# One decoder block on one core: order of the last block's cross-attention softmax, and who splits the experts' weights

## What is computed

```
x = x + attention(layernorm(x))            # 16 heads, rotary, softmax over 64 keys
x = x + cross_attention(layernorm(x), ctx) # 16 heads, ctx is (32, 64, 64)
x = x + experts(layernorm(x))              # 8 experts, top 2
```

```
scores = einsum('bhsr,bhlr->bhsl', q_r, k_r)
attn   = softmax(scores, axis=-1)
ctx_c  = einsum('bhsl,bld->bhsd', attn, kv_r)
out    = (ctx_c @ w_kc_kv per head) @ Wo.T
...
for i in range(8):
    h = silu(x @ Wg[i]) * (x @ Wu[i])
    output += w_i * (h @ Wd[i])            # w_i is 0 unless expert i is in the token's top 2
```

## Time and profile before

| | us |
|---|---|
| median of 3 runs | 747.36 |
| lowest and highest of the 3 | 743.05, 750.27 |
| profiled execution, its own time | 745.28 |
| its span | 743.5 |
| TensorE matmul busy | 649.7 (87% of the span) |
| VectorE busy | 532.6 (72%) |
| ScalarE busy | 332.5 (45%) |
| GpSimd busy | 230.4 (31%) |
| mean granted TensorE clock, share of full | 0.955 |

### The profile page before, as it was taken

How to read it: one execution, slowest core, us unless ns; L and a number is a source line. 1 busy time by engine, 2 the same in 40 slices (tenths; PEclk the granted TensorE clock), 3 DMA queues, 4 the chain that set the end, 5 groups by cost and what they waited for, 6 DMA issues and landing times.

```text
span 743.5 us, 14956 instructions
## 1 busy us (share of the span) xinstructions
PE 649.7 (87%) x5522; PEld 475.2 (64%) x5522; DVE 532.6 (72%) x1231; ACT 332.5 (45%) x991; POOL 230.4 (31%) x211
## 2 busy tenths in 40 slices
PE   3787999988999999999799997899889887998770
PEld 2466777777786666656666566566555775887660
DVE  4997999995687889478984789936879554443462
ACT  1476999996721135112351123502476453443330
POOL 1121000000027427232385423943253004003454
PEclk9997999997999999999989999999989999999895
DMA  8799900000000000000002000020442223334445
GB/s 300 148 374 420 408 6 2 1 2 2 2 15 15 1 2 2 15 1 1 2 15 82 18 1 1 23 78 2 126 153 72 70 80 114 100 107 120 130 120 177
DMA packets 49910, 61.52 MB, mean 83 GB/s; under 512 B 15536, under 2 KB 42416, under 8 KB 49584
## 3 DMA queue, kind: packets, MB, share of 16 engines
q1 hardware_dynamic: 45104, 50.88, 20.8%
q0 software_dynamic: 3072, 8.39, 3.6%
q10 hardware_dynamic: 1664, 1.31, 0.6%
HBM read 29.37 MB, written 31.20 MB: 81 GB/s over the span
## 4 chain that ended last, share of the span: by engine, by line
PE 64%; DVE 16%; ACT 7%; issue 6%; DMA 3%; POOL 1%; another core or an unknown queue 1%; ACTq 0%; SPq 0%; DVEq 0%; POOLq 0%
PE bank L352 55%; PE bank L361 9%; DVE m L1097 5%; DVE qmax L1311 2%; DVE csum L1320 2%; ACT kbd L1471 1%; ACT vbd L1457 1%; DMA lncol<-in_L_attn_ln_kv_b 1%; DMA gb<-slots,index 1%; ACT ex L1481 1%; DVE qc L1328 1%; ACT xth L1437 1%; POOL slots L1752 1%; DMA slots<-mxhat,index 0%
## 5 line engine op out<-in xcount | busy, mean ns | idle before, releaser
L1097 DVE TENSOR_TENSOR m<-bank,cst 128x512 f32<-128x512 f32 x192 | 120.9, 682 | 36.2 <-PE bank L352 34.6
L1738 POOL TENSOR_TENSOR r<-m,m 128x512 f32<-128x512 f32 x72 | 91.4, 1293 | 121.4 <-DVE m L1097 97.4
L352 PE MATMUL bank<-xth,wbh 128*128 128x512 f32 x192 | 80.8, 421 | 10.1 <-DVE m L1097 10.1
L1593 ACT ACTIVATE ex<-bank,nmax 128x64 f32<-128x64 f32 x256 | 56.0, 334 | 63.7 <-DVE nmax L1314 63.4
L352 PE MATMUL bank<-xtl,wbh 128*128 128x512 f32 x192 | 76.1, 396 | 0.0
L352 PE MATMUL bank<-xth,wbl 128*128 128x512 f32 x192 | 76.1, 396 | 0.0
L1580 ACT ACTIVATE qc<-bank 128x512 f32<-128x512 f32 x32 | 17.4, 596 | 101.0 <-PE bank L352 101.0
L352 PEld LDWEIGHTS bank<-wop,qc 128*128 128x128 f32 x256 | 46.6, 189 | 24.9 <-issue 19.5
L352 PE MATMUL bank<-wop,qc 128*128 128x256 f32 x256 | 62.3, 389 | 0.0
L352 PE MATMUL bank<-r,wqk 64*64 64x512 f32 x512 | 57.7, 594 | 0.0
L1481 ACT ACTIVATE ex<-bank,nmax 128x64 f32<-128x64 f32 x256 | 54.4, 356 | 3.0 <-DVE nmax L999 2.7
(11 more groups left out here) (217 smaller groups left out, 1493.3 us busy)
## 6 DMA issues: line engine op xcount, KB each, us to landing
slots<-cst SPq DMA_DIRECT2D x1, 13312.0 KB, 43.7
xs<-slots SPq DMA_DIRECT2D x46, 128.0 KB
slots<-ys SPq DMA_DIRECT2D x46, 128.0 KB
slots<-cst SPq DMA_DIRECT2D x1, 5120.0 KB, 50.3
wo_s<-in_L_xattn_Wo SPq DMA_DIRECT2D x1, 2048.0 KB, 18.1
wq_s<-in_L_xattn_Wq SPq DMA_DIRECT2D x1, 2048.0 KB, 11.8
wraw<-in_L_ffn_Wg SPq DMA_DIRECT2D x8, 256.0 KB, 4.7
wraw<-in_L_ffn_Wu SPq DMA_DIRECT2D x8, 256.0 KB, 5.0
```

The costliest lines, as they stand in the source:

```text
L352: return e.matmul(o, l, r, start=start, stop=stop, skip_group_check=True)
L1097: last = e.tensor_tensor(m4[n % 2][m][:, :].rearrange("p (b s) -> p b s", s=S), products[half][:, :].rearrange("p (b s) -> p b s", s=S), t ...
L1593: last = e.activation(ex[b % 4][:, (2 * n + odd) * 64:(2 * n + odd + 1) * 64], score_banks(b)[odd][:, n * 64:(n + 1) * 64], ACT.Exp, bias= ...
L1738: last = e.tensor_tensor(rope[n % 6][half][:, :], m4[n % 2][first][:, :], m4[n % 2][second][:, :], op)
```

## The change

Only block 3 and what follows it change; blocks 0 to 2 are issued as before.

- TensorE and ScalarE: in block 3 the transposes of batch `b` move from step `b + 3` to `b + 2` and now stand behind the scores of that step (`LAG[3]` is 2). Contexts and output halves move one step forward, on TensorE and VectorE.
- ScalarE: the high halves are made in the order 0, 1, 2, 3, 5, 4, 7, 6 (`SPLIT_ORDER`), all of them ahead of `x_high(0)`.
- VectorE: low halves of 2, 3, 4 and 6 at steps 8 to 11. Those of 5 and 7 go to GpSimd, at steps 11 and 12, behind its last scatter. A low half waits for the high half's place in `SPLIT_ORDER`.

```diff
+        LAG = (3, 3, 3, 2)
+        SPLIT_ORDER = (0, 1, 2, 3, 5, 4, 7, 6)
+        HIGH_AT = {8: (2,), 9: (3, 5), 10: (4, 7), 11: (6,)}
...
-                for s in range(12):
-                    if 3 <= s < 11:
+                lag = LAG[blk]
+                for s in range(9 + lag):
+                    if lag == 3 and 3 <= s < 11:
                         cross_weights_T(blk, s - 3)
                     if s < 8:
                         cross_scores(blk, s)
                     if s == 1 and blk:
                         route_step(blk - 1, 12)
-                    if s >= 4:
-                        contexts(blk, s - 4)
+                    if lag == 2 and 2 <= s < 10:
+                        cross_weights_T(blk, s - 2)
+                    if s > lag:
+                        contexts(blk, s - lag - 1)
                     if s < AHEAD - 1 and blk < 3:
                         half_products(blk + 1, s + 1)
-                    if s >= 6:
-                        cross_out(blk, OUT_AT[s - s % 2], s % 2)
+                    if s >= lag + 3:
+                        cross_out(blk, (s - lag - 3) // 2, (s - lag - 3) % 2)
...
             def weights_low(n):
                 at = slice(WE * n, WE * (n + 1))
-                w.wait_ge(w_hi, n + 1)
+                w.wait_ge(w_hi, SPLIT_ORDER.index(n) + 1)
                 e.tensor_tensor(wlo[:, at], wraw[:, at], whi[:, at].bitcast(F32), ALU.subtract).then_inc(w_lo, 1)
...
-                    if 4 <= s < 12:
-                        context_out(blk, s - 4)
-                    if s - 2 in OUT_AT:
-                        cross_out(blk, OUT_AT[s - 2])
+                    if 0 <= s - LAG[blk] - 1 < 8:
+                        context_out(blk, s - LAG[blk] - 1)
+                    if s - 2 + 3 - LAG[blk] in OUT_AT:
+                        cross_out(blk, OUT_AT[s + 1 - LAG[blk]])
                     if s == 2 and blk:
                         route_step(blk - 1, 13)
                     if blk == 3 and s == 8:
                         table(0)
-                    if blk == 3 and 9 <= s < 13:
-                        weights_low(s - 7)
+                    if blk == 3 and 8 <= s < 12:
+                        weights_low((2, 3, 4, 6)[s - 8])
...
             x_low(0)
-            weights_low(6)
             cross_out(3, 3)
             x_low(1)
-            weights_low(7)
...
-                    if 3 <= s < 11:
+                    if blk < 3 and 3 <= s < 11:
                         cross_weights_T(blk, s - 3)
                     if s < 8:
                         cross_exp(blk, s)
-                    if blk == 3 and 8 <= s < 12:
-                        weights_high(s - 6)
+                    if blk == 3 and 2 <= s < 10:
+                        cross_weights_T(blk, s - 2)
+                    if blk == 3 and s in HIGH_AT:
+                        for n in HIGH_AT[s]:
+                            weights_high(n)
...
-            weights_high(6)
             x_high(0)
-            weights_high(7)
             x_high(1)
...
                     if blk and 4 <= s < 12:
                         scatter(blk - 1, s - 4)
+                    if blk == 3 and s >= 11:
+                        weights_low((5, 7)[s - 11])
```

More of the change, by code:

```diff
@@ L1753, in scatter, with weights_low @@
                                      in_=mxhat[:, t, :], in_offset=None).then_inc(d_scat, 16)
+            def weights_low(n):
+                at = slice(WE * n, WE * (n + 1))
+                w.wait_ge(w_hi, SPLIT_ORDER.index(n) + 1)
+                e.tensor_tensor(wlo[:, at], wraw[:, at], whi[:, at].bitcast(F32), ALU.subtract).then_inc(w_lo, 1)
             def cross_normed(blk, b):
```

## The result

| | before | changed |
|---|---|---|
| median, us (16 runs each) | 748.56 | 754.39 |
| lowest and highest | 742.17, 754.73 | 749.62, 760.85 |
| profiled execution: span | 743.5 | 755.5 |
| first scores of block 3 at | 533.42 | 537.96 |
| last output half of the loop ends | 570.47 | 577.09 |

The changed kernel is slower. The medians are 5.8 us apart (0.78%); the ratio estimated from all runs is 1.0093, 95% interval 1.0065 to 1.0122, which is 6.9 us.

The account below looks back on a forecast made before the run. It took TensorE's queue and VectorE's low halves, ending close together, to bound the start of the expert rows. Softmax order 0, low halves 4.3 and clock 1.6 gave +5.9 us: 751.2, set up to 751.5; range 748.5 to 753.5, wide 743.8 to 755.5.

Parts of the forecast that it names:

- forecast case: VectorE's and GpSimd's low halves block each other, first tile's output product in time; 751.5 us, chance 0.50.
- TensorE's softmax order: Block 3's loop: work only moves; gain at most 0.66 us and a wait of about 0.8 cancel to 0.
- Scores later: Batch 7's scores come later in block 3; last scatter and first tile's load 0 to 2.8 us later, covered by low halves.
- GpSimd's price: A GpSimd low half of 1536 elements takes 3.75 us, three times its addition of 512 elements.
- No overlap of the five low halves: Before the expert rows, VectorE's three and GpSimd's two low halves add up, ending at 581.25; first `gate_up` 4.3 us later.
- rival A: VectorE's and GpSimd's low halves don't hinder each other; first `gate_up` at 576.3, a gain of 1.5 us; chance 0.15.
- Who goes first: Whether GpSimd's low halves start before VectorE's low half 3, holding up batch 7's copy; both expected at about 568.5.
- rival B: GpSimd goes first and keeps its place between its low halves, delaying VectorE's copy and TensorE's product; +8.9 us, chance 0.25.
- The clock: TensorE idles some 4 us before the first `gate_up`, so its granted clock falls; loss 1.6 us, 0 if idle under 3.
- Rival C: Earlier softmax transposes keep TensorE at full clock from 540 to 546, worth about 3 us; total 748.3, chance 0.10.
- After that: Expert rows, block 3's routing and the combine hang on the first tile and move as a whole.
- The chances: Whole run: slower by over 1% 0.28, faster by over 1% 0.02, within 1% 0.70.

Follow-up runs that it names:

- e1: Against the kernel before, only block 3's softmax order changed, all low halves staying on VectorE; stage 46.77 us against 44.33, ratio 1.0040.
- e7: Changed kernel with GpSimd's two low halves replaced by memsets of the same size, which write and read nothing; stage 44.24 us against the changed kernel's 51.11.
- e10: Changed kernel with each of GpSimd's two low halves made in three pieces of 512 elements; stage 51.99 us against the changed kernel's 51.11.
- e5: Changed kernel with GpSimd's low halves delayed until VectorE's low half 4 is already running; stage 48.87 us against the changed kernel's 51.11.
- e3: Changed kernel with low halves 5 and 7 given back to VectorE; stage 47.71 us against the changed kernel's 51.11, ratio 1.0007 to the kernel before.
- e6b: Changed kernel with GpSimd's low halves waiting so that it and VectorE take turns; stage 48.54 us against 51.11, ratio 1.0025 to the kernel before.
- e9: e3's kernel with the row table moved from step 8 to step 7 on VectorE; stage 55.73 us, ratio 1.0143 to the kernel before.
- e4: Changed kernel with batch 7's context copy ahead of low half 3 on VectorE; stage 49.52 us against 51.11, ratio 1.0073 to the kernel before.

## Why the prediction was right or wrong

The sum came near: +5.9 us forecast, +5.8 between the medians (6.9 by the ratio, 6.8 in the stage). The measured 754.39 is 2.9 above the forecast of 751.5 and beyond the forecast case's own 748.5 to 753.5; only the wide range, 743.8 to 755.5, holds it. And what agreement there is came partly by luck: errors that offset each other, in a case that I had not called likeliest.

*TensorE's softmax order, taken as 0, with ends -0.7 and +1.5.* **This step failed.** The loop grew by 2.1 us, beyond my upper end. "Since TensorE is 97% busy from 549 to 570.5, the sum of its work sets the end" rested on the order of before: the new one puts scores behind contexts, exponentials start later, and transposes wait for `ssb` copies, 0.36 and 1.04 us (e1: 1.0 us in the loop). These waits stand at 13.2 and 16.3 us of the stage, about where the stretch that I had read only begins (15.6). The second part, the context copy of batch 6 behind the table and a low half, I had at 0.8 and it is 0.91; I then cancelled it against a gain that never came. My own sign for this step, a loop that ends unchanged at 570 to 571.5, says the same: 577.09 is 572.55 in before's times (less the 4.54 us that were there already).

*Scores later.* I had the last scatter and the first load 0 to 2.8 us later. The scatter ends 3.6 us later in the stage (36.21 against 32.66), and so do the first tile's transposes begin. As I had it, this is covered in the changed kernel, and decides once the low halves are out of the way (e7).

*GpSimd's price, 3.75 us.* It is 3.42 in a row (3.43 to 3.47 for a single one). The Trainium skill's "GPSIMD Engine Reference" ("3.1 Elementwise — side-by-side cycle accounting"), whose figures scale to an estimate of 3.37, was nearer than three times the row for 512 elements; e10's pieces, 7.39 us for six against 6.84 for two whole ones, show what the cutting adds.

*No overlap of the five low halves.* Right: 3 x 1.75 + 2 x 3.42 = 12.1 us, and from 574.19 to the end of the last at 586.93 it is 12.7. So rival A, no interference, is out. e7 shows that it is GpSimd's reading that counts, and e5 that the waiting goes both ways, which I had only supposed from one scatter.

*Who goes first.* **This step failed too.** I gave half the chance to the case in which the context copy of batch 7 isn't held up, a quarter to rival B. Both instructions were issued together, as the working had it (568.5 and 568.0 to 568.9), and GpSimd's pair went through undivided: B, with its 8.48 us low half. B's price was set too high, 8.9 for a measured 6.8, although the low half began 1.15 us later in the stage than in its working. The output product at the lower clock took 5.77, not 7, since the clock was back before it ended, and no slow stretch was left behind it.

*The clock, 1.6 us.* The size is about right (5.77 - 3.62 = 2.15) but it fell in front of the output product and not in front of `gate_up`. The length of the idle stretch in front of `gate_up` was no safe sign either ("0 if the idle stretch stays under 3"): after 2.78 us in e3 and 2.63 in e5 `gate_up` started slow (0.79), after 2.79 in the kernel before, 2.63 in e6b and 2.79 in e9 it did not (0.49).

*Rival C, a gain on the softmax.* It is out: the clock stands at 0.50 from 544 to 550 us in the changed kernel, as it did from 540 to 546 before.

*After that, the rows move as a whole.* Right: 165.8 against 166.4 us from `gate_up` to the end.

*The chances.* I put 0.70 on a change within 1%, and called 1% about what a measurement tells from no change. The measured 0.93% is within 1%, and the interval of 16 runs is 0.3% wide to either side, so the slowdown is clear. For a forecast of 0.4 to 0.8% the text should have said that it would show as slower, instead of reading everything within 1% as no change.

## What to carry to other kernels

Before elementwise work on SBUF goes from VectorE to GpSimd, look what VectorE runs beside it: if that has two SBUF inputs, as here, the work isn't done in parallel, it is added, at GpSimd's rate (here 3.42 us for 1.75), and what is queued behind the held-up instruction waits as well. Look for gaps in VectorE's own queue first: one low half moved into a gap of 2.3 us, with its high half, gave 2.6 us, where two given to GpSimd lost 5.5 with the old order of the softmax. In a profile compare durations with the same line's median: in these traces the waiting shows as a long instruction, not as idle time. And when a stage is measured up to an instruction, look whether that instruction itself runs at full clock: e4's gain of 1.6 us was 0.5 seven tiles later.

## What the runs showed of the hardware that I had not expected

GpSimd instructions that stood ready one behind the other kept VectorE's two-input instruction out until the last of them: two of 3.42 us (8.48 us in all for VectorE's), and six of 1.26 us (9.02). It isn't always so. In e5, where GpSimd's first had itself been waiting, VectorE got in between. Both outcomes are already in the earlier trace rows: at 475.03 a VectorE instruction with one input (0.17 us by its line's median) waited for both of GpSimd's sums, 2.52 us, while the product issued at 55.33 was through at 56.67, 1.1 us before GpSimd's second addition ended (57.81). What decides stays open.

Scatters wait as well. Their median is 1.01 us. In all the kernels here, 15 scatters of the cross attention took 1.57 to 2.54 us, and each of them was issued while a VectorE low half was running and ended 0.82 to 0.89 us after that low half had ended: 574.17 against 573.34 in the changed kernel, 576.65 against 575.81 in e9. So a scatter is held to the end of a low half that came first. The eleven that were issued 0.23 to 0.75 us ahead of a low half took 0.96 each, and those low halves kept their 1.75 or 1.76. The Trainium skill, "SBUF — State Buffer", section "Who interferes with whom", says, as an inference, that a two-input instruction doesn't starve descriptor generation; the runs here say that it delays it, and the measurement decides.

This is also why the two engines met so exactly in the changed kernel. GpSimd's last scatter was held until 0.83 us behind the end of low half 2; VectorE, with a copy and an addition in between, issued low half 3 0.85 us behind it.

A GpSimd memset of 1536 elements (1.39 us) leaves VectorE's two-input instruction beside it at its 1.75 us, in agreement with what the same section says of instructions that only write.
